# One load instead of four for a head group's keys, in the self-attention phases of a fused transformer stack

## The reference

```
q, k, v = x @ Wq + bq, y @ Wk + bk, y @ Wv + bv      # y = x (self) or the context (cross)
scores  = einsum('bqhd,bkhd->bhqk', q, k) / sqrt(8)
attn    = softmax(scores)
x       = x + gate * (einsum('bhqk,bkhd->bqhd', attn, v) @ Wp + bp)
```

## Time and profile before

| | |
|---|---|
| median of 3 runs | 6443.32 us (6440.67 to 6449.58) |
| the profiled execution, its own time | 6443.67 us |
| its span, first to last instruction | 6441.9 us |
| PE busy | 5740.2 us, 89% of the span |
| ACT busy | 4218.4 us, 65% |
| DVE busy | 4122.9 us, 64% |
| POOL busy | 985.5 us, 15% |
| mean granted TensorE clock | 0.971 |
| key loads in self phases (`KP<-scr_ks`) | 512 DMAs, 36.0 KB each |
| key loads in cross phases (`KP<-scr_k`) | 768 DMAs, 225.1 KB each |
| query loads (`QP<-scr_q`) | 960 DMAs, 48.0 KB each |

### The profile page before, as it was taken

The page is one execution under the profiler, slowest core; times in us unless marked ns, Lnnn a source line. Parts: engine busy times, 40 slices in busy tenths (PEclk is TensorE's granted clock), DMA queues, the critical chain, the costliest instruction groups (busy, mean ns, idle before and its releaser), DMA issues.

```text
span 6441.9 us, 195420 instructions
## 1 busy us (share of the span) xinstructions
PE 5740.2 (89%) x73336; PEld 3375.8 (52%) x73336; DVE 4122.9 (64%) x6523; ACT 4218.4 (65%) x8158; POOL 985.5 (15%) x1660
## 2 busy tenths in 40 slices
PE   5999999999777899999999877779999999999998
PEld 3555555555444455555555344445555555555565
DVE  5777777777444677777777344457777777764443
ACT  3777777777655677777777555557777777773333
POOL 3122122121111111111111011122122112200000
PEclk9999999999888999999999988889999999999999
DMA  2221222221111221222222011122222222220110
GB/s 89 80 70 59 79 70 59 79 70 56 44 52 52 87 76 60 79 82 71 70 71 75 6 52 51 54 71 60 79 73 64 72 82 67 62 67 21 54 55 27
DMA packets 262059, 410.34 MB, mean 64 GB/s; under 512 B 28513, under 2 KB 172945, under 8 KB 260881
## 3 DMA queue, kind: packets, MB, share of 16 engines
q1 hardware_dynamic: 261392, 400.06, 21.2%
HBM read 316.81 MB, written 83.14 MB: 62 GB/s over the span
## 4 chain that ended last, share of the span: by engine, by line
PE 73%; ACT 8%; DVE 6%; issue 6%; SPq 2%; DMA 2%; POOL 1%; ACTq 0%; DVEq 0%; POOLq 0%
PE bank L1084 27%; PE bank L1192 17%; PE pair L1084 16%; ACT P L1328 3%; DVE MX L1492 3%; DMA QP<-scr_q 2%; PE pair L1179 2%; SPq L1035 1%; PE bank L699 1%; PE bank L690 1%; PE pair L626 1%; ACT QP L1339 1%; DVE ST L1449 1%; PE pair L463 1%; PE pair L722 1%
## 5 line engine op out<-in xcount | busy, mean ns | idle before, releaser
L1328 ACT ACTIVATE P<-bank 128x512 f32<-128x512 f32 (+1 forms) x5504 | 3090.0, 598 | 1297.3 <-PE bank L1084 1248.5
L1492 DVE TENSOR_REDUCE MX<-pair 128x2 f32<-128x802 f32 x3072 | 2918.8, 987 | 1108.4 <-PE pair L1084 1090.8
L1084 PE MATMUL bank<-QP,KP 128*32 128x256 bf16 (+2 forms) x25600 | 2147.0, 274 | 204.3 <-ACT P L1328 152.0
L1084 PE MATMUL pair<-KP,QP 96*32 96x401 bf16 (+2 forms) x16198 | 1785.6, 335 | 210.1 <-DMA QP<-scr_q 167.8
L1192 PE MATMUL bank<-P,VA 128*25 128x256 f32 (+1 forms) x22016 | 1762.1, 390 | 11.1 <-ACT RS L1334 9.5
L1084 PEld LDWEIGHTS bank<-QP,KP 128*32 128x32 bf16 (+2 forms) x25600 | 1026.9, 98 | 1331.0 <-ACT P L1328 644.6
L1084 PEld LDWEIGHTS pair<-KP,QP 96*32 96x32 bf16 (+1 forms) x16198 | 724.3, 98 | 356.3 <-DMA QP<-scr_q 161.0
L1192 PEld LDWEIGHTS bank<-P,VA 128*25 128x25 f32 (+1 forms) x22016 | 517.3, 103 | 462.9 <-issue 273.9
L1496 DVE TENSOR_REDUCE MX<-pair 128x4 f32<-128x1024 f32 x256 | 312.9, 1223 | 424.4 <-PE pair L1084 422.8
L1617 POOL COPY VA<-VN 128x416 f32<-128x416 f32 (+1 forms) x320 | 140.4, 439 | 2513.3 <-PE bank L1192 1300.2
L1339 ACT CAST QP<-pair 2x512 bf16<-2x512 f32 x640 | 339.4, 576 | 132.7 <-PE pair L1179 127.1
(11 more groups left out here) (242 smaller groups left out, 4293.5 us busy)
## 6 DMA issues: line engine op xcount, KB each, us to landing
KP<-scr_k SPq DMA_DIRECT2D x768, 225.1 KB
QP<-scr_q SPq DMA_DIRECT2D x960, 48.0 KB
CN<-ctx_n SPq DMA_DIRECT2D x40, 768.0 KB
scr_k<-KSF SPq DMA_DIRECT2D x48, 600.8 KB, 3.3
scr_k<-KSF SPq DMA_DIRECT2D x48, 600.0 KB, 3.3
CT<-ctx_t SPq DMA_DIRECT2D x24, 800.5 KB, 4.4
KP<-scr_ks SPq DMA_DIRECT2D x512, 36.0 KB
scr_q<-QS SPq DMA_DIRECT2D x80, 192.0 KB, 2.1
```

Of the source, the lines that this page charges most:

```text
L1084: last = nc.tensor.matmul(out[c:c + m, :], lhsT[:, c:c + m], rhs, start=start, stop=stop)
L1328: nc.scalar.activation(P[v % 2][0:kt, half * 2 * N:(half + 1) * 2 * N], SC[half][0:kt, :], ACT.Exp, scale=SCALE).then_inc(sem("probs_full" ...
L1492: nc.vector.tensor_reduce(MX[:, r, c:c + 2], MP[j % 2][:, :].rearrange("p (t k) -> p t k", t=2)[:, :, 0:SPANS[0][1]], AX.X, ALU.max).then_ ...
```

## The change

In the self phases one DMA loads a group's whole key pack, 72 rows of 1024 keys, instead of four DMAs of 72 rows of 256 keys. The four heads of a group lie side by side both in `scr_ks` and in `KP[g]`, so a row becomes one run of 2048 bytes where there were four of 512. The same bytes move. The semaphore of a group counts 64 for an element of a self phase (one key load and three query loads), and stays at 112 in cross phases. Cross phases, query loads and every other instruction are as before.

```diff
-            **{"packed_loaded%d" % g: 112 for g in range(NG)}), B)
+            **{"packed_loaded%d" % g: 112 if self.cross else 64 for g in range(NG)}), B)
...
-                    for h in range(G):
-                        sp.dma_start(KP[g][0:R9, h * ph.nk:(h + 1) * ph.nk],
-                                     kscr[:, G * g + h, :].unsqueeze(1).to_broadcast([3 * HD, 3, ph.nk])).then_inc(
+                    heads = 1 if ph.cross else G
+                    for h in range(0, G, heads):
+                        sp.dma_start(KP[g][0:R9, h * ph.nk:(h + heads) * ph.nk],
+                                     kscr[:, G * g + h:G * g + h + heads, :].rearrange("r h k -> r (h k)").unsqueeze(
+                                         1).to_broadcast([3 * HD, 3, heads * ph.nk])).then_inc(
                             sem("packed_loaded%d" % g), 16)
...
-                    pe.wait_ge(sem("packed_loaded%d" % g), at("packed_loaded%d" % g, b, 112))
+                    pe.wait_ge(sem("packed_loaded%d" % g), at("packed_loaded%d" % g, b, ph.c.per["packed_loaded%d" % g]))
```

## The result

The changed kernel takes 6334.93 us (median of 4 runs, 6331.62 to 6341.07) against 6443.46 us for the kernel before in the same series (4 runs, 6440.67 to 6449.58). The ratio is 0.9833, with a 95% interval of 0.9822 to 0.9845. The profiled execution took 6341.07 us (span 6338.2) and is the slowest of the four, so sums over the trace come out some 6 us short of the difference of the medians. The source lines behind line 1035 stand two lines lower in the changed kernel: 1084 is now 1086, and the query load 1039 is 1041.

A forecast was written before the change was run, and what follows sets the result against it. PE's wait for group 0's packs, once per self-phase element, was taken as the bound, with SP's issuing of seven DMAs on the loop. 74.7 + 5.7 + 27.5 = 107.9 us off 6443.67 gave 6335 us, range 6316 to 6372.

The forecast's parts named there:

- (1): Self phases, group 0: query loads start 2.41 us earlier behind one key load, shortening all 31 PE waits, 74.7 us.
- C: Rival for the self-phase loads: transfer, not issue, sets the landing, so nothing changes; 6443 or up to 6430 us; chance 0.07.
- D: Rival for the self-phase loads: one long key load blocks the queries behind it, so slower, 6506 us; chance 0.06.
- (2): Self phases, groups 1 to 3: loads are issued sooner but not waited for today, so they give nothing.
- (3): End of s2: SP reaches the load of c2's context sooner, ending VectorE's wait, 5.7 us (bounds 0 and 5.7).
- (4): Slots 6 and 7 of self-phase elements: two in three keep PE's full clock, 1.37 us each, 27.5 us (bounds 0 and 41).
- Rival B: Self phases: the wait shrinks but PE loses the clock in nearly each element, 6363 to 6378 us; chance 0.21.

The follow-up runs named there:

- The run with group 0 alone: Against the kernel before, one key load only for group 0 of a self phase, groups 1 to 3 keep four: 6344.42 us, ratio 0.9847.

## Why the prediction was right

**(1) The load wait.** Right, by its own numbers. 31 x 2.41 = 74.7 us were predicted, the wait shrank by 129.6 - 53.8 = 75.8 us. The single key load takes 0.82 us, as worked out from four equal steps, the last query load 2.46 us to free PE, and 1.43 us of wait stay where 1.42 were predicted. The run with two loads lies between, with 0.8 to 0.9 us for each DMA. The bytes are the same in all three kernels and the landing takes as long, so it is SP's issuing. The rule of the Trainium skill ("DMA: Bandwidth & Descriptors", Issuing engines are not separate DMA queues), by which the sequencer's part is usually small, does not hold for these DMAs, of which SP needs 767 to 785 ns each, while the line needs 0.9 us for all 147 kB of a group's keys at 162 GB/s.

That the keys don't hold the queries up was taken at nothing, with 0.9 us as a bound. It is next to nothing: the last query load frees PE after 2.46 us, against 2.42 before, and in the window behind the key issue the line moves 162 GB/s, where the four loads of before gave 46 and 53:

```profile
1732.00:1733.00 1.00, 0.61 (x8) 0.42 (x8) 0.18 (x2) 0.33 (x2) 0.00 (x0) 1.00 0.44 162
```

With it and the time itself rivals C and D fall. The 50 GB/s were the pace at which SP issued, not that at which the line moves.

**(2) Groups 1 to 3.** "They give nothing" was true of the kernel before and not quite of the changed one. The run with group 0 alone is 9.5 us above the changed kernel. By the traces it loses 4.1 us at the end of s2 (70.0 us against 65.9 from the last load wait to c2's first), which the prediction has as (3), and 14.8 us in the 28 elements, less what its unchanged stretches gained by chance. Part of the 14.8 are the waits of 0.3 to 0.4 us for group 1 (in s1 PE waits 24 times and 24.9 us for loads there, against 15 times and 21.5 us), which arise only because (1) and (4) let PE come earlier.

**(3) The end of s2.** 5.7 us were predicted, 5.3 measured from the last load wait of s2 to c2's first, and VectorE's wait is gone.

**(4) The clock.** Two in three elements were taken to keep it, at 1.37 us each; 20 of 30 do, and an element takes 28.34 us where the clock falls and 26.85 where it is kept, against 28.3 and 26.9. That the same gap of 1.4 us goes both ways was an estimate between two rows, and that it came out to the element is luck in part: why it falls in every third element of s1, and not in more or fewer, the prediction could not say. Rival B, that it falls nearly each time, fails by the count. What the prediction passed over is that the term does not stand by itself. Kept in the kernel before, where 41 us were to be had by it, the clock gave 17, and the load of group 1 appeared as the next wait. Kept at this gap in the changed kernel it gave nothing, since it then fell at the other gap; with both filled it gave 16.2 us in the 28 elements (9 by the medians), near the 13.5 that a third of 41 would be. So the price of a lost clock was right, and the gap that takes it was not the only one. And the 27.5 us were had only together with the single loads of group 1. With group 0's alone the 28 elements are 79.5 us shorter than before (864.2 to 784.7), of which 28 x 2.41 = 67.5 are term (1), and 12 are left for the clock.

**The sum.** 107.9 us were predicted off the profiled execution, which gave 102.6 (6443.67 - 6341.07); the medians differ by 108.5. By stretches: 94.3 us in 28 elements, which by the terms are 28 x 2.41 + 28 x 0.67 x 1.37 = 93.2.

## What to carry to other kernels

Count the DMAs that an issuing engine puts ahead of the one that is waited for. Each load of 72 rows cost SP 0.77 to 0.82 us here, with rows of 512 to 12808 bytes, and the wait for the last one fell by 0.8 us for each that was merged away. Merge only where the loads are small and waited for, and check each phase apart: the same edit cost 97 us where a load has 900 KB. A gain on such a loop is real only as far as the next load and the clock follow: the full clock, for which 41 us were counted, was worth 17 by itself, since the next group's load was then the one waited for.

## What was not expected of the hardware

- How many packets are under way at once went with a DMA's rows: 12 for 72 rows read from 24, 6 for 18 rows read from 6. With rows of 12808 bytes they moved 149 and 108 GB/s. Cut by columns into four DMAs, the same keys moved at 166 GB/s.
- Packets of 12808 bytes took 858 ns where those of 3202 bytes took 185, both 12 at once: by the estimate 179 and 208 GB/s.
- With key loads of 900 KB PE stops 31 times, 51.6 us, in the middle of matmuls on the same tiles, often in every second element at the same instruction (4480.34, 4676.53, 4870.81, 5065.64 and 5260.68 us, about 195 us apart). The stops of over 0.5 us end 1.3 to 1.7 us after a packet of the queue `instruction` has landed, 26 times in 26. What holds that packet back beside these loads is open; that it was an instruction PE waited for is what the trace suggests, and no run tests it. The packets of that queue take 1.1 us in the mean in both kernels.
- A gap of 1.4 us in PE's work took the clock in 10 of 30 cases, and once it was filled the clock fell in 8 of 15 elements of s1 at a gap of 1.7 us, which had cost it in none of them.
- A matmul with a 128x256 moving tile in f32 runs as two passes of 0.22 us.
